# Layer 3 attention: the transfers of the maxima's rows issued by GpSimd ahead of a tile's finish, and the statistics of a finished tile moved to the fourth quad

## The reference, cut to what matters

```
# x: (64, 64, 256) after the layers before; ctx_2048: (64, 64, 256)
def _L3_xattn_ref(q, k, v, gamma):           # q = layernorm(x), k = v = ctx
    N_HEAD = 8
    B, Dq, Lq = q.shape                      # 64, 64, 256
    qh = q.reshape(B, 8, 8, 256); kh = k.reshape(B, 8, 8, 256); vh = v.reshape(B, 8, 8, 256)
    scale = 1.0 / jnp.sqrt(8)
    qk = jnp.einsum('bhdq,bhdl->bhql', qh, kh) * scale   # 256 x 256 for each of 8 heads
    sm = jax.nn.softmax(qk, axis=-1)
    ret = jnp.einsum('bhql,bhdl->bhdq', sm, vh)
    return gamma * ret.reshape(B, Dv, Lq)
...
x = x + _L3_xattn_ref(_layernorm(x, axis=-1), ctx_2048, ctx_2048, L3_xattn_gamma)
x = x + _L3_ffn_ref(_layernorm(x, axis=-1), ...)
```

## Time and profile before

| What | Value |
|---|---|
| Time before, median of 3 runs | 2152.83 us (2148.16 to 2154.12) |
| Profiled execution, its own time | 2155.54 us |
| Its span in the profile | 2153.7 us |
| Busy: PE, PEld, DVE, ACT, POOL | 1773.0, 1333.7, 1517.8, 979.8, 955.5 us |
| DMA moved | 182.39 MB, mean 85 GB/s |
| Transposed scores of layer 3 attention (line 2768) | first start 1413.7 us, last 1795.7 us |

### The profile page before, as it was taken

The page is one execution under the profiler, slowest core; times in us unless marked ns, Lnnn a source line. Parts: engine busy times, 40 slices in busy tenths (PEclk is TensorE's granted clock), DMA queues, the critical chain, the costliest instruction groups (busy, mean ns, idle before and its releaser), DMA issues. The chain is left out here.

```text
span 2153.7 us, 42587 instructions
## 1 busy us (share of the span) xinstructions
PE 1773.0 (82%) x14235; PEld 1333.7 (62%) x14238; DVE 1517.8 (70%) x3683; ACT 979.8 (45%) x2343; POOL 955.5 (44%) x1091
## 2 busy tenths in 40 slices
PE   6989846299797699889898789878888886989993
PEld 5869712188575577777777568644444442557772
DVE  7975842286757699898998756688888983544446
ACT  3743131034323355454554335358777875523330
POOL 2420016543338366666666485314434443743330
PEclk9989956599898699999999889879999998989996
DMA  7831026530205000000000201037777764333337
GB/s 230 272 106 62 11 76 175 143 127 6 72 1 162 1 1 0 0 0 0 0 0 0 52 9 45 17 63 150 146 145 152 153 123 109 112 100 105 107 105 249
DMA packets 150747, 182.39 MB, mean 85 GB/s; under 512 B 40193, under 2 KB 132593, under 8 KB 146481
## 3 DMA queue, kind: packets, MB, share of 16 engines
q1 hardware_dynamic: 140769, 158.05, 28.4%
q0 software_dynamic: 9808, 22.23, 3.5%
HBM read 121.78 MB, written 56.79 MB: 83 GB/s over the span
## 5 line engine op out<-in xcount | busy, mean ns | idle before, releaser
L2867 DVE TENSOR_REDUCE mx<-bank 128x2 f32<-128x512 f32 x512 | 315.4, 679 | 24.6 <-PE bank L2746 22.5
L2839 ACT ACTIVATE e<-bank 128x512 f32<-128x512 f32 x512 | 280.4, 599 | 88.4 <-PE bank L2768 81.6
L1914 POOL TENSOR_TENSOR q_l<-q_l,rot_l 64x512 f32<-64x512 f32 x128 | 162.2, 1267 | 130.9 <-DVE rot_l L2112 130.9
L2783 PE MATMUL bank<-e,val 128*32 128x256 f32 x2048 | 165.2, 395 | 9.4 <-ACT nd L2834 8.8
L2768 PEld LDWEIGHTS bank<-q,k 64*128 64x128 f32 x1024 | 77.8, 188 | 135.7 <-ACT e L2839 79.3
L2768 PE MATMUL bank<-q,k 64*128 64x256 f32 x1024 | 130.6, 333 | 26.7 <-DMA q<-rows 22.6
L2746 PE MATMUL bank<-k,q 62*128 62x256 f32 x1024 | 112.7, 300 | 22.1 <-DVE mx L2867 16.5
L1946 PE MATMUL bank<-qcT,wq_abs 96*128 96x128 f32 x1024 | 127.3, 284 | 0.0
L3054 POOL DMA_INDIRECT y<-y,y_row x71 | 69.0, 972 | 127.2 <-DVE y L3329 122.3
L1946 PEld LDWEIGHTS bank<-qcT,wq_abs 96*128 96x128 f32 x1024 | 121.3, 198 | 2.6 <-issue 0.2
L1971 PE MATMUL bank<-wvo,rd_l 128*128 128x256 f32 x512 | 116.4, 381 | 0.0
(11 more groups left out here) (445 smaller groups left out, 4749.1 us busy)
## 6 DMA issues: line engine op xcount, KB each, us to landing
k<-k_parts SPq DMA_DIRECT2D x128, 128.0 KB, 5.2
q<-q_parts SPq DMA_DIRECT2D x64, 256.0 KB, 4.3
got<-rows SPq DMA_DIRECT2D x71, 129.0 KB, 2.1
k_parts<-k_parts_a SPq DMA_DIRECT2D x64, 128.0 KB, 3.1
moe_rows<-zero_a SPq DMA_DIRECT2D x16, 512.0 KB
w<-in_e0w SPq DMA_DIRECT2D x16, 512.0 KB, 3.9
q_parts<-parts SPq DMA_DIRECT2D x64, 128.0 KB, 2.7
rec<-rec_rows SPq DMA_DIRECT2D x64, 128.0 KB, 2.5
```

What stands on the lines that cost most here:

```text
L1914: nc.gpsimd.tensor_tensor(q[64:P, j, four(m), :], q[64:P, j, four(m), :], rot[64:P, j, four(m), :], ALU.add).then_inc(s["rope_added"], 1)
L2783: last = nc.tensor.matmul(readout[32 * g:32 * g + 32, side], val[:, a.n % 2, g, i, lt, :], e[:, slot(i, r), lt, :], start=(i == 0 and lt = ...
L2839: nc.scalar.activation(e[:, slot(i, r), :, :].rearrange("p k n -> p (k n)"), scoresT(i, r)[:, :], ACT.Exp).then_inc(s["exp_ready"], 1)
L2867: v.tensor_reduce(mx[:, a.n, r % 2, 0, at:at + 2], scores(r)[:, :].rearrange("p (a n) -> p a n", a=2), AX.X, ALU.max, negate=True).then_in ...
```

## The change

Two things are moved. `lay_rows`, with its wait for `rows_ready` and its two transfers, leaves SyncE's program and stands in GpSimd's, after `split_max` of tile a+1 and ahead of `finish` of tile a-3. `stats` of tile a-3 on VectorE moves from the place after the unit (1, 3) to the place after the unit (3, 1). The transfers themselves, their sizes and their semaphores are the same.

```
--- before.py
+++ after.py
@@ -2596,15 +2596,6 @@
                 sp.dma_start(vt[:, a.n, :, :], c.d["ctx_cols"][bass.ds(a.t, 1)].rearrange(
                     "a p k n -> p (a k) n")).then_inc(s[vt_loaded[a.n]], 16)
 
-            def lay_rows(a):
-
-                sp.wait_ge(s["rows_ready"], tile_ready(a.t))
-                settle(sp, s["sp_passed"])
-                for b, base in enumerate(BASE3):
-                    at = slice(base + TOP_ROW3, base + TOP_ROW3 + 2)
-                    sp.dma_start(whole(q[at, a.n, :]),
-                                 whole(rows[4 * H3 * b:4 * H3 * b + 4 * H3, a.n, :])).then_inc(s[rows_loaded[a.n]], 16)
-
             def gather(a):
 
                 b = a.n % 2
@@ -2635,8 +2626,6 @@
                         [2 * H3, DQ3, D])).then_inc(s[rec_loaded[b]], 16)
 
             def tile(a):
-                if a.exists(1):
-                    lay_rows(a.to(1))
                 if a.exists(-2):
                     store_inverse(a.to(-2))
                 if a.exists(AHEAD):
@@ -2650,7 +2639,6 @@
                     settle(sp, s["sp_passed"])
                     load(a.to(BUF))
 
-            lay_rows(At(0, 0))
             run(sp, tile)
             end = At(NT // BUF - 1, BUF - 1)
             store_inverse(end.to(-1))
@@ -2705,6 +2693,15 @@
                 nc.gpsimd.tensor_tensor(parts[:, b, 1, :], xq[:, b, :], whole(parts[:, b, 0, :]),
                                         ALU.subtract).then_inc(s["low_ready"], 1)
 
+            def lay_rows(a):
+
+                pool.wait_ge(s["rows_ready"], tile_ready(a.t))
+                settle(pool, s["pool_passed"])
+                for b, base in enumerate(BASE3):
+                    at = slice(base + TOP_ROW3, base + TOP_ROW3 + 2)
+                    nc.gpsimd.dma_start(whole(q[at, a.n, :]),
+                                 whole(rows[4 * H3 * b:4 * H3 * b + 4 * H3, a.n, :])).then_inc(s[rows_loaded[a.n]], 16)
+
             def finish(a):
                 b = a.n % 2
                 pool.wait_ge(s[rec_loaded[b]], 32 * (uses(a) + 1))
@@ -2721,6 +2718,8 @@
                     for r in range(4):
                         if (i, r) == (0, 1) and a.exists(1):
                             split_max(a.to(1))
+                        if (i, r) == (0, 2) and a.exists(1):
+                            lay_rows(a.to(1))
                         if (i, r) == (0, 2) and a.exists(-3):
                             finish(a.to(-3))
                         if (i, r) == (1, 3) and a.exists(1):
@@ -2730,6 +2729,7 @@
 
             values(At(0, 0))
             split_max(At(0, 0))
+            lay_rows(At(0, 0))
             run(pool, tile)
             for n in (3, 2, 1):
                 finish(At(NT // BUF - 1, BUF - n))
@@ -2889,7 +2889,7 @@
                             maxima(a.to(LEAD), i, r)
                         if (i, r) == (1, 1) and a.exists(-2):
                             invert(a.to(-2))
-                        if (i, r) == (1, 3) and a.exists(-3):
+                        if (i, r) == (3, 1) and a.exists(-3):
                             stats(a.to(-3))
                         if (i, r) == (0, 2) and a.exists(AHEAD):
                             norm(a.to(AHEAD))
```

More of the change, by code:

```diff
@@ L2597, in load @@
                     "a p k n -> p (a k) n")).then_inc(s[vt_loaded[a.n]], 16)
[L2599 to L2606, removed]
             def gather(a):
```

## The result

The changed kernel takes 2202.60 us (median of 4 runs, 2194.67 to 2215.86) against 2150.49 us for the kernel before on the same chip: ratio 1.0247, 95% interval 1.0217 to 1.0278. It is 52 us slower. The direction is the one forecast; the size is 2.7 times the 19 us of the forecast, and outside the range that I gave.

A forecast was written before the change was run, and what follows sets the result against it. It took SyncE's loop of 11.91 us a tile as the bound, replaced by a two-tile loop of 25.3 us, 12.65 a tile: +0.70 in 27 tiles, +18.9 us, so 2172 us, range 2149 to 2190.

The forecast's parts named there:

- SyncE's loop: SyncE's queue: one turn of 11.91 us paces the tiles; without the two issues, 1.58 us, it falls to 10.33.
- waits of the first view: TensorE's wait for rows, 22.6 us, and VectorE's for the finished tile, 29.6 us; said only to show where engines stood.
- The statistics at the new place: VectorE's statistics after unit (3, 1): costed at nothing, hidden by half a microsecond; old place would cost several microseconds a tile.
- a loop over two tiles: GpSimd's wait for copied rows delays low part, store and load of q and k: 25.3 us for two tiles.
- The signs that I named for it: On TensorE: wait for rows gone, a wait for q and k of about 1.4 us in a tile instead.
- The two issues 2.26 us: GpSimd's two transfers of rows, taken as 0.98 + 0.30 + 0.98 us, with ends of 1.45 and 3.08.
- The load 9.03: Load of q and k, first issue to last landing: 9.03 us, long because the DMA engines are already full.
- Start of the tile to the end of the copy: 5.34: From the tile's start on TensorE to the end of ScalarE's copy of rows: 5.34 us in the two-tile sum.
- 12.65 us a tile: Half the two-tile sum of 25.3 us; replaces 11.95, so +0.70 in each of 27 tiles, +18.9 us.
- the last term: Plain scores on TensorE to the end of ScalarE's copy of rows: forecast 4.94 us.
- Late rows: Rival: GpSimd's rows land late amid the load; at 6.8 us landing a tile takes 13.5, +42 us, 2195; chance 0.07.
- GpSimd held up by VectorE while it issues: Rival: a GpSimd issue stands until VectorE's normalisation ends; at most +0.2 us a tile, 2177 us; chance 0.03.

The follow-up runs named there:

- e6: Kernel before with GpSimd's low part ahead of the finish and the statistics moved to the fourth quad, SyncE still issuing the rows; ratio 0.9998, 12.01 us a tile.
- e3: Changed kernel with GpSimd's low part of tile a+4 put ahead of the two transfers of rows; ratio 0.9905, 11.32 us a tile.
- e1: Kernel before with only the statistics moved from after unit (1, 3) to after (3, 1); ratio 1.0002.
- e2: Changed kernel with the statistics put back after unit (1, 3); ratio 1.0567, 16.56 us a tile.
- e4: Kernel before with the statistics moved; GpSimd waits for the copied rows and fills memory for 1.9 us, SyncE issues the rows; ratio 1.0228.
- e9: Changed kernel with six idle matmuls on TensorE ahead of each tile's wait for its rows; ratio 1.0180, 13.23 us a tile.
- e12: Kernel before, statistics moved, GpSimd only waiting for the copied rows, four idle matmuls ahead of TensorE's wait for rows; ratio 1.0072, 12.47 us a tile.
- e11: Kernel before with ScalarE issuing the rows right behind its copy and the statistics in the fourth quad; ratio 1.0194, 13.36 us a tile.

## Why the prediction was right and wrong

- *SyncE's loop sets the pace before, 1.58 us of it go.* Right. e6 (SyncE keeps the issues) stays at 12.01, e3 (it doesn't) runs at 11.32.
- *TensorE's and VectorE's waits of the first view are not what the stage is worth.* Right for VectorE: e1, 1.0002.
- *The statistics at the new place cost nothing, at the old one several microseconds a tile.* Right in sign and near in size: e2 is 2.7 us a tile slower than the changed kernel. At the new place VectorE's wait was still 17.6 us in the stage.
- *The low part, the store and the load hang behind GpSimd's wait, a loop over two tiles.* Right: e4 has the loss with nothing but the hold, e3 is rid of it when the low part goes ahead, and from 1536.22 on the tiles come in pairs. The signs that I named for it were half wrong: TensorE's wait for the rows did not go but doubled (48.1 us), and the wait for q and k was 11.5 us in 8 tiles, not 1.4 in each.
- *The two issues 2.26 us.* Too long. They took 1.25, each 0.61 on the median, with 0.70 between the copy and the first where I had 0.1. Together 1.97 against 2.36.
- *The load 9.03.* 9.99 in the turn that was walked, and 9.99 on the mean of the eight turns that end with a wait for k.
- *Start of the tile to the end of the copy: 5.34.* This is the step that failed. I took it from a tile that TensorE entered after a wait of 1.07 at the full clock. The loop makes one tile of each pair wait for both; TensorE then stands 3 to 5 us, its clock falls to 0.50, and from the plain scores on the term grows to 7.64 in the turn that was walked and to 6.73 on the mean of eight, against 4.94. The prediction has no word on the clock: it let a wait cost its own length and nothing behind it. Here the wait also slowed the next link of the loop that it came from.
- *12.65 us a tile.* 13.86 measured, 1.21 more, or 2.4 for two tiles. Over the eight turns the last term gives 1.79 of them (6.73 against 4.94), the load 0.96, the issues with their gap -0.39: 2.36 together. The first is the largest, and it stands in the stretch where the matmuls ran at the clock of 0.50. e9 bounds it from below by an experiment: without the low clock 0.63 of the 1.21 are gone, with its own idle work still inside. Not settled is what sets the long tiles at nearly the full clock: in e12 10 of the 27 tiles take 12.0 and the others 12.1 to 14.6, with 10.0 us of waiting for rows in 16 of them.
- *Late rows, held for a rival with 0.07.* They were seen (landings up to 8.2, 48.1 us of waiting), in 15 of TensorE's 23 waits they alone were the last to arrive, and the price of +42 us was nearer to the result (+52) than my +19. As a cause by itself it fell with e3 and e4: the rows are late where the load is late. That its price came near is in part luck, as it too was added up at the full clock.
- *GpSimd held up by VectorE while it issues.* Not seen: the 64 issues took 594 to 788 ns. But it was not put to the test: VectorE's normalisation had ended at least 2.9 us ahead of every issue, and what VectorE did during the issues was to take maxima (line 2867). From the Trainium skill's "SBUF — State Buffer", section "SBUF: two separate sides", I had estimated an issue 2.5 us longer; no run here shows such a stretch, and the changed kernel could not, since the two never overlap in it.

## What to carry to other kernels

Taking two issues off a queue that sets the pace is worth its length, but the engine that takes them over must be able to wait there: ask what is queued behind the new wait, and put ahead of it whatever another queue waits for (here one step moved turns +2.5% into -1%). When a loop spans two tiles, add it up for two, expect the wait to gather in one of them (here after six tiles), and price the links that follow a long wait of TensorE at the clock that it has after standing still, not at the clock of a tile that ran through: here that was 1.4 to 2.6 us in a paying tile, and in e11 some 1.5.

## What the runs showed of the hardware

A pair of direct transfers of 16 KB issued by GpSimd took 1.25 us, 0.61 each, less than the 0.98 of the indirect ones in the trace of before, and less than SyncE's 1.45 for the same pair. Ahead of the first stood 0.70 us after the end of the copy that released it, while memory filling released by the same semaphore in e4 began 0.15 after it (1615.34 to 1615.49).

After TensorE had stood 3.4 us its granted clock was 0.50 from 1612 to 1617 us. In e11, where it stood 1.65 us, it was 0.57 from 1628 to 1632; one tile earlier it had stood 1.52 us (until 1614.18) and the clock stayed at 1.00. Over the 27 tiles of e11, waits of 1.51 to 1.54 us stand in tiles with the slow matmuls and in tiles without them, so the length of one wait does not tell whether the clock falls.
